# Local attention in four blocks of 64 queries, its probabilities divided before the transpose, in a step written out by hand

## The reference

```
def local_attention(q, k, v):                      # 8 heads of 64, WINDOW = 64
    bq = q.reshape(b, h, w, WINDOW, d) * QK_SCALE
    bk, bv = (look_around(bk), look_around(bv))    # the block before and the own block
    sim = jnp.einsum('bhwid,bhwjd->bhwij', bq, bk)
    mask = (i < j) | (i > j + WINDOW) | (j == -1)
    attn = jax.nn.softmax(jnp.where(mask, -jnp.finfo(sim.dtype).max, sim), axis=-1)
    out = jnp.einsum('bhwij,bhwjd->bhwid', attn, bv)

def _layer(x, ...):
    h = shift_token(x)                             # half of the channels one token later
    q, k, v = jnp.split(h @ wqkv, 3, axis=-1)
    q, k = rotary_xpos(l2norm(q) * qs, l2norm(k) * ksc)
    x = x + local_attention(q, k, v) @ wo
    h = layernorm(shift_token(x)) @ w1 + b1        # then a * gelu(g), and @ w2
    return x + (a * gelu(g)) @ w2 + b2
```

## Time and profile before

| | |
|---|---|
| runs | 1995.65, 1996.06, 1997.3 us; median 1996.06 |
| profiled execution | 1996.95 us, its span 1995.2 us |
| instructions | 33260 |
| busy | PE 1725.4, PEld 1412.0, DVE 1382.1, ACT 979.5, POOL 454.4 us |
| first local part, residual of step 0 to that of step 15 | 648.8 to 1105.7 us |
| second local part, the same | 1526.0 to 1972.5 us |
| residual of step 14 in the two parts | 1082.0 and 1949.3 us |
| first score matmul of step 0, first part | 621.2 us |

### The profile page before, as it was taken

The page is one execution under the profiler, slowest core; times in us unless marked ns, Lnnn a source line. Parts: engine busy times, 40 slices in busy tenths (PEclk is TensorE's granted clock), DMA queues, the critical chain, the costliest instruction groups (busy, mean ns, idle before and its releaser), DMA issues.

```text
span 1995.2 us, 33260 instructions
## 1 busy us (share of the span) xinstructions
PE 1725.4 (86%) x10812; PEld 1412.0 (71%) x10875; DVE 1382.1 (69%) x3623; ACT 979.5 (49%) x2591; POOL 454.4 (23%) x344
## 2 busy tenths in 40 slices
PE   6999989666466999999989899999968999999997
PEld 5888887334255777777777687777757777777776
DVE  4678768788956767768686565455547677687683
ACT  2354454332124565665656544434215756656654
POOL 1210010000013334334252100000013343343340
PEclk9999999676678999999999999999869999999999
DMA  4000000000010000000000000000000000000000
GB/s 143 1 1 0 0 0 1 0 1 0 0 53 1 4 3 1 3 4 3 3 1 3 2 1 0 0 0 0 0 0 3 3 1 3 3 3 4 3 1 24
DMA packets 15113, 13.87 MB, mean 7 GB/s; under 512 B 11286, under 2 KB 14138, under 8 KB 14650
## 3 DMA queue, kind: packets, MB, share of 16 engines
q1 hardware_dynamic: 15034, 12.88, 2.0%
HBM read 9.74 MB, written 1.05 MB: 5 GB/s over the span
## 4 chain that ended last, share of the span: by engine, by line
PE 50%; DVE 32%; issue 12%; ACT 5%; POOL 1%; DVEq 1%; POOLq 0%; ACTq 0%
PE bank L1653 7%; PE bank L1673 4%; PE bank L1784 4%; DVE arena_ffn L985 3%; DVE arena_attn L1000 3%; PE bank L1685 3%; DVE ssq L993 3%; PE bank L1822 3%; PE bank L1771 3%; DVE probT L725 3%; PE bank L1664 3%; DVE arena_ffn L981 3%; PE bank L1842 2%; PE bank L1826 2%; DVE nmaxF L718 2%
## 5 line engine op out<-in xcount | busy, mean ns | idle before, releaser
L556 POOL TENSOR_TENSOR arena_ffn<-arena_ffn 128x1024 f32<-128x1024 f32 x60 | 141.3, 2355 | 506.0 <-DVE arena_ffn L985 506.0
L725 DVE COPY probT<-bank 128x512 f32<-128x512 f32 x288 | 196.7, 683 | 35.5 <-PE bank L1664 35.2
L552 POOL TENSOR_TENSOR inv<-ssq,mhalf 128x16 f32<-128x16 f32 x64 | 186.3, 2911 | 76.3 <-DVE ssq L994 76.0
L1673 PE MATMUL bank<-vF,probT 128*128 128x64 f32 x1536 | 195.8, 270 | 4.9 <-DVE probT L725 2.9
L1673 PEld LDWEIGHTS bank<-vF,probT 128*128 128x128 f32 x1536 | 186.5, 192 | 11.9 <-DVE probT L725 11.6
L1653 PE MATMUL bank<-arena_setup 128*128 128x192 f32 (+1 forms) x1024 | 174.1, 304 | 7.1 <-ACT arena_setup L1419 5.5
L718 DVE TENSOR_REDUCE nmaxF<-bank 128x2 f32<-128x384 f32 (+1 forms) x192 | 114.6, 597 | 92.0 <-PE bank L1653 92.0
L1653 PEld LDWEIGHTS bank<-arena_setup 128*128 128x128 f32 x1024 | 157.1, 194 | 12.8 <-issue 1.2
L1471 ACT ACTIVATE arena_conv<-bank,nmaxF 128x192 f32<-128x192 f32 x256 | 105.6, 419 | 114.8 <-DVE nmaxF L718 111.3
L1362 ACT ACTIVATE prob<-bank,nmax 128x128 f32<-128x128 f32 (+1 forms) x256 | 90.1, 421 | 118.2 <-DVE nmax L718 90.1
L540 POOL TENSOR_TENSOR rstd<-var,mhalf 128x2 f32<-128x2 f32 x24 | 17.0, 710 | 534.2 <-DVE var L680 534.2
(11 more groups left out here) (271 smaller groups left out, 4132.3 us busy)
## 6 DMA issues: line engine op xcount, KB each, us to landing
packF<-in_packF SPq DMA_DIRECT2D x1, 3122.0 KB
arena_history<-in_packG SPq DMA_DIRECT2D x1, 2560.0 KB, 9.9
HS<-XH SPq DMA_DIRECT2D x32, 63.5 KB
X<-in_x_tiled SPq DMA_DIRECT2D x1, 1024.0 KB, 5.0
out_dram<-X SPq DMA_DIRECT2D x8, 128.0 KB, 1.9
arena_setup<-in_const_masks_a SPq DMA_DIRECT2D x1, 512.0 KB, 5.4
arena_setup<-in_const_masks_f SPq DMA_DIRECT2D x1, 512.0 KB
HS<-XH SPq DMA_DIRECT2D x32, 0.2 KB
```

Of the source, the lines that this page charges most:

```text
L552: pool.tensor_tensor(inv[:, t, :, 0], ssq[:, t, :, 0], mhalf[:, 0:16], ALU.pow).then_inc(sems["inv_ready"], 1)
L556: pool.tensor_tensor(t1[:, t], t1[:, t], t2[:, t], ALU.add).then_inc(sems["rope_sum"], 1)
L725: dve.tensor_copy(probT[:, u % 2], bank[4 + u % 2][:]).then_inc(sems["pt_copied"], 1)
L1673: ins = pe.matmul(o, probT[:, u % 2, n * P:(n + 1) * P], val, start=first, stop=(kt == keys // P - 1), skip_group_check=True)
```

## The change

Attention goes in four units, one for each block of 64 queries, with all eight heads in each. The stationary operand of a score matmul now holds the 64 queries of two heads (`qZ`, in block-diagonal form), the moving one the two key blocks of that pair of heads (`kT`): 128 columns. The probabilities are divided by their sums on VectorE before they are transposed (`weigh`, which replaces `output`: in place on `prob`, an SBUF tile). The value matmul has the values as its stationary operand, and so gives the transposed result at once: the transposes of the result are gone. `take_yT` now takes, per unit, two pieces of 64 partitions, and for the middle block ScalarE puts together a tile of values (`middle_values`). VectorE still copies the transposed probabilities (`attn_copy`).

The order of a step is new on TensorE, VectorE and ScalarE. The second half's `scaled`, `transpose_qk` and `take_qkT` move from the end of the step before to the beginning of the row's own step. GpSimd's and SyncE's queues keep their order (but for one memset less).

```diff
-F_FROM = (0, P - F_WINDOW)
-F_UNITS = 6
+F_UNITS = T // F_WINDOW
+F_KEYS = (slice(0, 3, 2), slice(0, 3, 2), slice(1, 3), slice(1, 4, 2))
+F_MASK = (0, 1, 2, 1)
...
@@ vector: win_close, win
-                for t in range(NT):
-                    scaled(v, 0, t)
+                scaled(v, 0, 0)
...
-                def output(t):
-                    dve.wait_ge(sems["pv_done"], v.at("pv_done", i, (2, F_UNITS)[t]))
-                    ch.link(dve.reciprocal(rdenF[:, t], denF[:, t]))
-                    dve.tensor_tensor(yF[:, t].rearrange("p (h d) -> p h d", d=FHD), bank[6 + t][:].rearrange("p (h d) -> p h d", d=FHD),
-                                      rdenF[:, t].broadcast_to([P, FH, FHD]), ALU.mult).then_inc(sems["y_ready"], 1)
-
-                for s in range(F_UNITS + 2):
...
+                def weigh(u):
+
+                    dve.wait_ge(sems["exp_ready"], v.at("exp_ready", i, u + 1))
+                    ch.link(dve.reciprocal(rdenF[:, u], denF[:, u]))
+                    pr = prob[:, u % 2].rearrange("p (c k) -> p c k", k=P)
+                    dve.tensor_tensor(pr, pr, rdenF[:, u].broadcast_to([P, 4, P]), ALU.mult).then_inc(sems["norm_ready"], 1)
+
+                scaled(v, i, 1)
+                attn_max(v, i, 0, 4, P, nmaxF, F_SCORE_BANKS)
+                if hid:
+                    hidden_stats(*hid)
...
+                weigh(1)
+                attn_max(v, i, 3, 4, P, nmaxF, F_SCORE_BANKS)
+                weigh(2)
+                if m:
+                    mlp_end(m[0], m[1])
+                attn_copy(v, i, 1)
+                weigh(3)
+                attn_copy(v, i, 2)
+                if nxt:
+                    norms(vn, ni, 1, sch)
+                attn_copy(v, i, 3)
+                if hid:
+                    hidden_apply(*hid)
+                if nxt:
+                    scaled(vn, ni, 0)
                 if fin:
                     final_stats(m[0], m[1])
+                local_residual(v, i, l)
@@ scalar
+            def middle_values(v, i):
...
+            def take_yT(v, i, u):
+                act.wait_ge(sems["pv_done"], v.at("pv_done", i, u + 1))
+                for j in range(2):
+                    rows_ = slice(64 * j, 64 * j + 64)
+                    ins = act.activation(yTF[rows_, u // 2, :, 64 * (u % 2):64 * (u % 2) + 64],
+                                         bank[6 + u % 2][rows_].rearrange("p (c j k) -> p c j k", j=2, k=64)[:, :, j], ACT.Copy)
+                ins.then_inc(sems["yT_ready"], 1)
@@ tensor
+            def local_scores(v, i, u):
...
+                for c in range(4):
+                    ins = pe.matmul(b[:, c * P:(c + 1) * P].rearrange("p (a k) -> p a k", a=2),
+                                    qZ[:, u, c].rearrange("p j k -> p (j k)"), kT[:, c, F_KEYS[u]],
+                                    start=False, stop=True, skip_group_check=True)
...
+            def transpose_probs(v, i, u):
+                if u == 0:
+                    pe.wait_ge(sems["qkT_ready"], v.at("qkT_ready", i, NT))
+                pe.wait_ge(sems["norm_ready"], v.at("norm_ready", i, u + 1))
...
+            def weigh_values(v, i, u):
...
+                for c in range(4):
+                    ins = pe.matmul(bank[6 + u % 2][:, c * P:(c + 1) * P], values[:, c * P:(c + 1) * P],
+                                    probT[:, u % 2, c * P:(c + 1) * P], start=True, stop=True)
...
+                local_scores(v, i, 0)
+                if nxt:
+                    project_qk(vn, ni, nl, 0)
...
+                transpose_qk(v, i, 1)
+                if nxt:
+                    project_qk(vn, ni, nl, 1)
+                transpose_probs(v, i, 0)
+                local_scores(v, i, 2)
+                if m:
+                    hidden_out(*m)
+                pe.wait_ge(sems["down_used"], v.at("down_used", i, 0))
+                weigh_values(v, i, 0)
+                local_scores(v, i, 3)
+                transpose_probs(v, i, 1)
+                transpose_probs(v, i, 2)
```

More of the change, by code:

```diff
@@ L391, in zeros_by @@
         def zeros_by(n):
-            return N_POOL_FILL + sum((plan[m] == "conv") + 2 * (plan[m] == "win" and plan[m - 1] != "mlp")
+            return N_POOL_FILL + sum((plan[m] == "conv") + (plan[m] == "win" and plan[m - 1] != "mlp")
                             for m in range(n + 1))
@@ new lines, in win @@
+                scaled(v, i, 1)
[3 more added lines that the diff above has]
+                if nxt:
+                    rope_part(vn, ni, nl, 0, 0)
+                attn_max(v, i, 1, 4, P, nmaxF, F_SCORE_BANKS)
+                if nxt:
+                    rope_part(vn, ni, nl, 0, 1)
+                if m:
+                    gated(*m)
+                weigh(0)
+                if nxt:
+                    norms(vn, ni, 0, sch)
@@ L1438, in win_close @@
                 take_values(v, 0)
-                for t in range(NT):
-                    take_qkT(v, 0, t)
+                take_qkT(v, 0, 0)
             def gelus(v, i, l):
@@ L1464, in win @@
                     prime(ACT.Exp, 1)
-                for u in range(F_UNITS):
-                    t, heads, keys = attn_unit(u, 2)
-                    act.wait_ge(sems["max_ready"], v.at("max_ready", i, u + 1))
-                    act.wait_ge(sems["pt_ready"], v.at("pt_ready", i, u - 1))
-                    width = keys - F_FROM[t]
-                    for k, hh in enumerate(heads):
-                        ins = act.activation((prob, probW)[t][:, u % 2, (k + 1) * keys - width:(k + 1) * keys],
-                                             bank[u % F_SCORE_BANKS][:, k * width:(k + 1) * width],
-                                             ACT.Exp, bias=nmaxF[:, u, k:k + 1], accum_out=denF[:, t, hh])
-                    ins.then_inc(sems["exp_ready"], 1)
-                    if nxt and u in (0, 3):
-                        squares(vn, ni, u // 3)
-                take_yT(v, i, 0)
+                local_exp(v, i, 0)
+                take_qkT(v, i, 1)
+                if nxt:
+                    squares(vn, ni, 1)
+                local_exp(v, i, 1)
+                middle_values(v, i)
+                take_yT(v, i, 0)
+                local_exp(v, i, 2)
+                local_exp(v, i, 3)
+                take_yT(v, i, 1)
+                take_yT(v, i, 2)
+                if hid:
+                    take_hidden(hid[0], hid[2])
+                take_yT(v, i, 3)
                 if nxt:
@@ L1700, in project_values, with project_out @@
                           start=True, stop=True).then_inc(sems["v_psum"], 1)
+            def project_out(v, i, l):
+                pe.wait_ge(sems["yT_ready"], v.at("yT_ready", i, F_UNITS))
+                for t in range(NT):
+                    for c in range(4):
+                        ins = pe.matmul(bank[6][:, t * P:(t + 1) * P], yTF[:, t, c], f_at[f"wo{l}"][:, c * C:(c + 1) * C],
+                                        start=(c == 0), stop=(c == 3))
+                ins.then_inc(sems["down_ready"], 1)
             def win_open(v, l):
@@ L1709, in win_close @@
                     project_values(v, 0, l, t)
-                for t in range(NT):
-                    transpose_qk(v, 0, t)
+                transpose_qk(v, 0, 0)
             def win(n, l, i):
@@ L1765, in win @@
-                transpose_y(1)
-                if nxt:
-                    transpose_qk(vn, ni, 1)
-                pe.wait_ge(sems["yT_ready"], v.at("yT_ready", i, NT))
-                for t in range(NT):
-                    for c in range(4):
-                        ins = pe.matmul(bank[6][:, t * P:(t + 1) * P], yTF[:, t, c], f_at[f"wo{l}"][:, c * C:(c + 1) * C],
-                                        start=(c == 0), stop=(c == 3))
-                ins.then_inc(sems["down_ready"], 1)
+                project_out(v, i, l)
```

181 lines of the change are left out of this document (85 added, 96 removed).

## The result

The changed kernel takes 2058.32 us (median of 4 runs, 2057.06 to 2060.09) against 1996.68: 1.0312 times as long, 95% interval 1.0298 to 1.0326. The profiled execution took 2057.06 us, its span is 2055.3 against 1995.2.

What follows compares the result with a forecast made beforehand. Neither engine alone was taken to bound the step: a chain passes from TensorE (9.8 us) to VectorE (20.6). Steps of 32.6 and 30.5, plus 12 per part for the clock, add 63: 2058 us predicted, own range 2036 to 2080.

Steps and rivals of the forecast that it cites:

- VectorE's work: VectorE's own busy time in a local attention step, claimed to fall from 22.55 to 22.0 us.
- The holds: GpSimd's additions hold the two-SBUF-input `weigh` multiply: 0.95 us for unit 0, 2.15 for unit 1, the latter gone in steps 10-14.
- the prediction's other reading: By the Trainium skill's rule, holds last to the addition's end: 0.14 us longer each, some 7 us on the whole.
- The shift: VectorE idles 4.3 us a step ahead of `hidden_stats` until SyncE's transfers land, 6.0 us behind the residual.
- No hold: Rival: the addition doesn't block the multiply, but shift and clock act; 29.5 us per step, 2009 us in all; chance 0.14.
- The residual: VectorE's idle ahead of the residual, behind TensorE's transposes and projection, stays at 3.1 us a step.
- the score: VectorE's short wait at the first maximum of a step, 0.07 us, entered as 0.1.
- The clock: TensorE's granted clock falls after its gaps: one low stretch in nearly every step, 0.8 us each, 12 per part.
- the sum: VectorE's work plus its waits per local step: 32.6 us against 30.4, or 30.5 in steps 10 to 14.
- The last step: Each local part's last step, without a next row: plus 4.3 us of shift, less some 2.3 of TensorE work, 25.4.
- The rest of the kernel: Everything outside the two local parts, opening aside: claimed untouched by the change.
- the opening with step 0: The opening gains 2.5 us through earlier scores, step 0 gets 2.8 more: 0.3 together per part.

Runs made afterwards that it cites:

- Experiment 1: Changed kernel, with the `weigh` multiply of units 1 to 3 reading a PSUM operand instead of the probabilities in SBUF (output differs): 2000.75 us, ratio 1.0028.
- Experiment 2: Changed kernel with `hidden_stats` moved from behind the first maximum to behind `weigh(0)` in VectorE's queue: 2016.27 us, ratio 1.0109.
- experiment 3: Changed kernel with both the PSUM operand for units 1 to 3 and `hidden_stats` behind `weigh(0)` (output differs): 1950.07 us, ratio 0.976.
- Experiment 4: Changed kernel with 22 transposes of the identity in TensorE's gap ahead of unit 1's transposes: 2066.16 us, ratio 1.0365.
- experiments 6 and 7: Changed kernel with VectorE's queue reordered a second time, first alone (2015.86 us, ratio 1.0089), then with TensorE's queue reordered too (1921.41 us, ratio 0.9613).
- experiment 10: Kernel before, with 12 transposes of the identity filling TensorE's 1.43 us gap in the last linear-attention row: 1985.24 us, ratio 0.9938.
- experiment 7: Changed kernel with VectorE's second reordering, and TensorE's value projections and unit 1's weighing ahead of unit 2's transposes: 1921.41 us, ratio 0.9613.
- experiment 30: No run of this number: the text says "the seventh experiment", then counts 30 multiplies. The run meant is experiment 7, 1921.41 us.
- experiment 9: Kernel before with `hidden_stats` moved right behind the first maximum of a step, nothing else: 2056.5 us, ratio 1.0289.

## Why the prediction was right, and which of its terms were not

The time, 2058.3, is within 0.3 us of the forecast. The terms aren't that good, and they add up to 2059 rather than 2058 (1996.95 + 63 - 0.9).

- **VectorE's work**: 22.0 predicted. Measured 25.16 less holds of 3.15 (0.99 + 2.16): 22.0.
- **The holds**: 0.95 and 2.15 predicted, 0.99 and 2.16 measured, gone from unit 1 in steps 10 to 14 as forecast. With 0.14 more each, the prediction's other reading, they would have been 1.09 and 2.29. Experiment 1 shows the cause. Steps 0 and 1 held unit 0 for 2.16 too, which I hadn't listed.
- **The shift**: 4.3 of idle predicted, 3.99 measured, landing 6.1 behind the residual (6.0). As a wait it was right. As a price it failed: "VectorE stands for 4.3 us, with everything in the step behind it" left out that 2.15 of it cover a wait for ScalarE's squares, which the list of waits didn't have. The omission doesn't show in a kernel that has the shift wait; it shows in experiment 2. By the same terms the queue of experiment 3, with no shift wait and one hold, should have been 22.0 + 3.1 + 0.1 + 0.95 = 26.2 and is 29.45. The rival *No hold*, 2009 us, was too slow: the kernel of experiment 1, which still has unit 0's hold, takes 2000.75, with 12 us less than before between the parts.
- **The residual** 3.1 predicted, 3.44 measured; **the score** 0.1 and 0.17.
- **The clock**: "one low stretch in nearly every step", 0.8. There are two, at 0.90 of granted clock, and step 6 takes 34.2 where the sum has 32.6 without the clock: 1.6. Experiment 4 takes about 1.0 of it away with the second stretch: there the wait of 0.76 ahead of the last copy is gone and that ahead of the residual is 3.08 for 3.44. This is the term that was mis-sized: steps 1 to 9 came out at 34.0 and 33.9 for 33.4, 10 us in the two parts, and steps 10 to 14 of the first part at 31.9 for 31.3, 3 us.
- **The last step**: 25.4 predicted, 27.8 and 28.8 measured. Experiment 2 has 26.7 and 25.4 there without the shift wait, so that wait is worth 1.1 and 3.4, and the 2.3 us of saved TensorE work did not come: even without the wait the step is longer than the 23.6 and 23.2 of before. The orders of experiments 6 and 7 give 25.4 and 23.8; what makes the difference was not looked for.
- **The rest of the kernel** "the change touches nothing else": the failed step. It touched nothing there, and yet 17.4 us went, 12.6 of them in the last row, where a low stretch of TensorE's clock disappeared; filling the gap in front of it takes 12 us off the kernel before (experiment 10). And the opening with step 0, put at 0.3 more, took 3.0 less in the first part, for a reason that was not looked for. Parts predicted at 483 each measured 493.6 and 490.3, 18 more; the linear attention gave 17.4 back. That the total was exact is luck.

The step's cause is settled: unit 1's hold and the shift together cost 108 us (experiment 3) against 62 of loss, with unit 0's hold still in. The change's own idea, four units instead of six with VectorE's work inside TensorE's stretch, is worth having once both queues fit it (experiment 7).

## What to carry to other kernels

Before placing a VectorE instruction that reads two SBUF tensors, look for GpSimd's long SBUF instructions in the same place: here it waited for the end of the addition, and an instruction with a PSUM operand or one SBUF input in that slot took its usual time (0.69 and 1.21 us). When a wait is added, ask which waits it covers, and when it is removed, which one is next; the difference is its price. Orders of two engines' queues go together: the last order on VectorE alone made the kernel 21 us slower than the one ahead of it, and with TensorE's queue adapted 94 us faster than that. And read the parts apart from the total: stages that an edit doesn't touch moved by up to 19 us.

## What the runs showed of the hardware

- A multiply with two SBUF inputs waited for the end of a GpSimd addition of 2.35 us (up to 2.16 us), ending 0.55 behind its recorded end. It did not wait for GpSimd's power of 128x16 elements, recorded as 2.91 us long: in the changed kernel `scaled` starts inside it 30 times, 0.4 to 2.4 us behind its start, and takes 1.21 or 1.22; in the seventh experiment 30 multiplies of `weigh` start 0.9 us behind its start and take 0.69. The Trainium skill (SBUF — State Buffer, "SBUF: two separate sides") has the hold last for the whole instruction; the addition agrees but for its last 0.14 us, the power's recorded length doesn't.
- TensorE's clock stayed at 0.50 for 34.1 us (1429.6 to 1463.7 in the kernel before), with TensorE recorded busy for 32.7 of them, and the same instructions behind the same gap of 1.43 us ran at 1.00 in the changed kernel. The stretch went in all nine kernels with the changed local attention, whose last instruction lies some 300 us ahead, and in the kernel before when that one gap was filled; it stayed in experiment 9.
- 2.6 us of useless matmuls in a gap of 2.9 us made a step 1.0 us shorter; in the steps without that gap they made it 2.4 us longer.
